# An attention mask taken off TensorE: GpSimd adds it to ScalarE's relu tile from step 5 on

## The chip, the cores and the metric

The kernel runs on one NeuronCore of one Trainium2 chip. The metric is the device time of one launch, in microseconds. Matmuls run on TensorE (PE), activations on ScalarE (ACT), elementwise work and reductions on VectorE (DVE) and GpSimd (POOL); SyncE (SP) issues the transfers.

## What is computed

128 graphs of 128 nodes with 256 features go through one graph attention layer (L0) and then a stack of three layers (L1), each attention, normalisation, a feed-forward of 256 to 1024 to 256, normalisation. The attention of L1 is, cut to what matters here:

```python
mask = adj + eye(n) > 0
scores = si[:, :, None] + sj[:, None, :] + attn_b[l]
scores = where(scores >= 0, scores, 0.2 * scores)
scores = where(mask, scores, -inf)
attn = softmax(scores, axis=-1)
agg = einsum('bij,bjd->bid', attn, x)
h = layernorm(x + agg, g1[l], beta1[l])
ff = gelu(h @ W1[l] + b1[l]) @ W2[l] + b2[l]
x = layernorm(h + ff, g2[l], beta2[l])
```

L0 has the same attention with the mask `adj == 0` and an elu behind it, between two residual sums.

## The kernel before

**Units and steps.** Four graphs form a group (T = 4; 32 groups), and a group in one of the three layers is a unit (96 units). Groups go in chunks of eight: eight groups in layer 0, the same in layer 1, then layer 2. So unit u has the layer u % 24 // 8. The program is one sequence of steps s from -6 to 97, each written by `body(st)` once for every engine; s = 24 to 71 is a hardware loop that turns twice over 24 steps. Each engine executes its own list in order; semaphores tie the lists together. Step s has the feed-forward of unit s and, around it, the attention of later units: the aggregation of unit s + 1, the scores and weights of unit s + 2, the row dots of unit s + 3, and the second normalisation of unit s - 1. The L0 work of a group is spread over four steps (`early`, `middle`, `late`, `end`); from group 8 on, `early` falls on every third step (s = 2, 5, 8, ... 71), `middle` on the next (3, 6, ... 72), `late` on the one after that. `only_middle(s)` is true in the steps of s % 3 == 0 from 3 to 72.

**The attention of a unit.** TensorE's `score_rows` turns the dots of the rows into a tile of sj in PSUM with four 128x128 fp32 transposes (L551) and adds the mask (0 or -2^100, bf16) with one matmul of the identity by the 128x512 mask tile (L553). ScalarE's `above` writes e = relu(4 (scores + si)) into SBUF (L724). VectorE's `row_lows` clears a column (L933), makes (scores + e) times -0.2 in PSUM and takes its minimum in each row (L936, four times). ScalarE's `exps` exponentiates from PSUM into e (L732); TensorE turns e (L559), and aggregates (L564). The leaky relu of score + si is 0.2 (x + relu(4x)) without the row's constant, which the softmax doesn't see.

**The feed-forward.** TensorE makes eight hidden blocks (`hidden(c)`, L588, six 128x512 matmuls each) in four PSUM banks. ScalarE takes the gelu twice (L859 rounded to g_hi, L861 in place), VectorE makes the remainder g_lo (`g_low(c)`, L983). Then TensorE makes the second product in four parts (`second(r)`, L605). The waits that tie them: `hidden(c)` for c >= 4 writes a bank again, and waits until its old block's g_lo is there; `turn = [0, 2, 3, 1, 2, 0, 3, 1]` gives the banks, so block 6 waits for g_lo 2 and block 7 for g_lo 3; and `second(0)` waits for g_lo c ahead of its block c.

**Order on the engines.** TensorE in a step: hidden(0), scores of s + 2, aggregation of s + 1 (L564), hidden(1), turn of L0's weights (if late), hidden(2), hidden(3), L0's scores (if middle), hidden(4) to (7), row turns (L646), second(0), second(1), L0's aggregation (if late), second(2), turn of e (L559), second(3). VectorE: g_low(0), row sums (L1037) and statistics, g_low(1), the variance (L968) of the first normalisation, `next_lows` (L933, L936), g_low(2), `first_norm` (L1074, waits for GpSimd's root), g_low(3), and so on to g_low(7), with the statistics of the input (in steps 2, 5, ...) and of vb (L957) in between; then low rows (L1108), shifts, and the row dots (L952). GpSimd: inverse root of the first normalisation (L1283), `scaled_rows` (L374, eight adds and products into hb), roots, the masks (`take_waits` L1278, then L1338 or L1347), L0's residual (L374 into elu_r), and last the affine part of unit s - 1 and, where its layer is the last, the residual (L374 into xo, 8 or 12 times). In steps 2, 5, ... that last part waits for the dots of the group (`dots0_ready`).

`take_waits(j)` is a one-column product into `spare` that takes up the waits ahead of a masking instruction. In steps 4 to 11 there are also pieces of late weights to split (`late_piece`).

Of the kernel before, what the change touches and what calls it, by code (L numbers as in the profile page):

```python
# [13 lines left out]
P = 128  # L14
T = 4
# [23 lines left out]
def build(nc, x, adj, w_fc, w_attn0, attn_w, attn_b, w1, b1, w2, b2, g1, beta1, g2, beta2, out):  # L39
# [25 lines left out]
    LATE = 4  # L65
    U = L * G
# [18 lines left out]
    with ctx:  # L85
# [27 lines left out]
        spare = sb("spare", [P, 4 + T])  # L113
# [111 lines left out]
        above_ready = sem("above_ready")  # L225
        low_ready = sem("low_ready")
# [38 lines left out]
        above0_ready = sem("above0_ready")  # L265
        low0_ready = sem("low0_ready")
# [55 lines left out]
        def early_norm(s):  # L322

            return s == -1

# [72 lines left out]
        def _(sp):  # L398
# [38 lines left out]
            def body(st):  # L437
# [90 lines left out]
        def _(pe):  # L528
# [18 lines left out]
            def score_rows(scores, mask, dot, done):  # L547


                for t in range(T):  # L550
                    pe.matmul(scores[:, t * P:(t + 1) * P], dot[:, 1, t:t + 1].to_broadcast((P, P)), ident[:, :],  # L551
                              is_transpose=True, start=(t == 0), stop=True, skip_group_check=True)
                pe.matmul(scores[:, :], ident_b[:, :], mask.rearrange("p t m -> p (t m)"),  # L553
                          start=False, stop=True, skip_group_check=True).then_inc(done, 1)
# [12 lines left out]
            def body(st):  # L567
# [51 lines left out]
                def next_scores():  # L619
                    if live(s + 2):  # L620
                        pe.wait_ge(dots_ready, st.nth(s + 2, 2 * T))
                        pe.wait_ge(m_in, 16 * st.nth(s + 2))
                        if live(s + 1):
                            pe.wait_ge(et_ready, st.nth(s + 1))
                        score_rows(ps_s, m1[s % 2][:, :, :], dots[s % 2], scores_ready)
# [6 lines left out]
                def first_scores():  # L632
                    if v1 is not None:
                        pe.wait_ge(dots0_ready, st.nth0(v1, 2 * T))
                        pe.wait_ge(masks0_ready, st.nth0(v1))
                        if v1:
                            pe.wait_ge(et0_ready, st.nth0(v1 - 1))
                        score_rows(ps_s0, m0[:, :, :], dots0, scores0_ready)
# [62 lines left out]
        def _(act):  # L701
# [40 lines left out]
            def body(st):  # L742
# [129 lines left out]
                next_exps()  # L872
                first_exps()
# [8 lines left out]
                second_norm()  # L882
# [8 lines left out]
        def _(dve):  # L891
# [37 lines left out]
            def row_lows(nth, u, taken, e, scores, lows, above_done, ready):  # L929


                dve.wait_ge(above_done, nth(u))
# [43 lines left out]
            def body(st):  # L976
# [9 lines left out]
                def first_lows():  # L986
                    if v1 is not None:
                        row_lows(st.nth0, v1, spare[:, 3 + T:4 + T], e0, ps_s0, low0, above0_ready, low0_ready)
# [56 lines left out]
                def first_variance():  # L1045
                    if live(s + 1):
                        if not live(s):
                            dve.tensor_copy(spare[:, 2:2 + T], neg_half[:, :])
# [38 lines left out]
                def input_variance():  # L1087
                    if v0 is not None:
                        if not live(s):
                            dve.tensor_copy(spare[:, 2:2 + T], neg_half[:, :])  # L1090
# [3 lines left out]
                def made_variance():  # L1094
                    if v3 is not None:
# [3 lines left out]
                        dve.tensor_copy(spare[:, 2:2 + T], neg_half[:, :])  # L1099
# [164 lines left out]
        def _(pool):  # L1264
# [38 lines left out]
            def body(st):  # L1303
# [29 lines left out]

                def mask():
# [33 lines left out]

                first_root()
# [49 lines left out]
```

## Time and profile before

| what | us |
|---|---|
| median of three runs | 2773.87 (2773.44 to 2774.45) |
| the profiled execution | 2771.33 |
| its span, first to last instruction | 2769.5 |
| TensorE busy | 2651.5 (96%), granted clock 0.985 |
| VectorE busy | 2138.1 (77%) |
| ScalarE busy | 2200.2 (79%) |
| GpSimd busy | 1689.8 (61%) |

The span holds all instructions of the profiled execution; 1.8 us of its time lie around it. Busy shares are means over the whole span, and matmuls overlap, so a sum of matmul durations is more than the busy time. In what follows a step begins at the first L588 matmul of its hidden(0): step 34 at 1073.70, 35 at 1102.14, 36 at 1129.11, 44 at 1350.04, 45 at 1377.32, 46 at 1405.22, 80 at 2338.39.

### The profile page before, as it was taken

How to read it: one execution, taken by the hardware profiler on the slowest of the kernel's cores; microseconds unless marked ns; L12 is line 12 of the kernel's file. 1: busy time of each engine (PE TensorE's matmuls, PEld its weight loads, DVE VectorE, ACT ScalarE, POOL GpSimd, SP SyncE). 2: the span in 40 equal slices, each digit the busy share in tenths (PEclk: the TensorE clock that was granted, in tenths of full speed). 3: DMA queues.
4: the chain of work that ended last, by engine and by line, in shares of the span. 5: the costliest groups of instructions: out<-in, count | busy, mean ns of one | idle time of the engine just before them, and what ended most of it. 6: DMA issues, size and time to landing. Idle time of an engine off the chain costs nothing.

```text
span 2769.5 us, 53308 instructions
## 1 busy us (share of the span) xinstructions
PE 2651.5 (96%) x16771; PEld 2386.7 (86%) x16868; DVE 2138.1 (77%) x7995; ACT 2200.2 (79%) x4494; POOL 1689.8 (61%) x2197
## 2 busy tenths in 40 slices
PE   3699999999999999999999999999999999999997
PEld 2488888988888989888888888889888998998997
DVE  5898878777878777878777878777878777676674
ACT  4699888888888888888887888888878777777774
POOL 4467666566766565566676666555677554454655
PEclk8699999999999999999999999999999999999999
DMA  5221322222222221122222122222222211111111
GB/s 177 90 70 62 95 81 92 66 79 76 87 81 77 66 71 62 64 70 88 85 90 69 65 67 76 69 68 68 80 89 91 62 45 52 35 52 52 51 64 54
DMA packets 118589, 203.43 MB, mean 73 GB/s; under 512 B 12800, under 2 KB 85536, under 8 KB 118304
## 3 DMA queue, kind: packets, MB, share of 16 engines
q1 hardware_dynamic: 118304, 199.97, 22.3%
q8 instruction: 137, 2.24, 0.3%
q14 instruction: 148, 1.21, 0.1%
HBM read 116.05 MB, written 83.89 MB: 72 GB/s over the span
## 4 chain that ended last, share of the span: by engine, by line
PE 71%; DVE 12%; POOL 8%; issue 5%; ACT 3%; DMA 0%; DVEq 0%; SPq 0%; POOLq 0%; ACTq 0%
PE bank L605 32%; PE bank L588 26%; PE ps_u L564 7%; POOL xo L374 3%; DVE g_lo L983 3%; DVE st L957 2%; PE ps_u L646 2%; POOL rs L1283 2%; DVE ub L1074 2%; PE ps_s L559 2%; PE ps_s L551 1%; POOL hb L374 1%; DVE vb L952 1%; DVE ub L952 1%; ACT g_hi L859 1%
## 5 line engine op out<-in xcount | busy, mean ns | idle before, releaser
L605 PE MATMUL bank<-w_hi,g_hi 128*128 128x256 f32 x3072 | 890.5, 290 | 15.3 <-DVE g_lo L983 15.1
L605 PE MATMUL bank<-w_hi,g_lo 128*128 128x256 f32 x3072 | 865.2, 282 | 0.0
L605 PE MATMUL bank<-w_lo,g_hi 128*128 128x256 f32 x3072 | 863.9, 281 | 0.0
L859 ACT ACTIVATE g_hi<-bank,b_eff 128x512 fp32r<-128x512 f32 x768 | 529.3, 689 | 334.4 <-PE bank L588 327.9
L983 DVE TENSOR_TENSOR g_lo<-bank,g_hi 128x512 fp32r<-128x512 f32 x768 | 518.9, 686 | 202.3 <-ACT bank L861 188.2
L588 PE MATMUL bank<-zt_hi,w_hi 128*128 128x512 f32 x1536 | 632.4, 412 | 12.0 <-DVE g_lo L983 5.6
L588 PE MATMUL bank<-zt_hi,w_lo 128*128 128x512 f32 x1536 | 607.7, 396 | 0.0
L588 PE MATMUL bank<-zt_lo,w_hi 128*128 128x512 f32 x1536 | 606.4, 395 | 0.0
L605 PEld LDWEIGHTS bank<-w_hi,g_hi 128*128 128x128 f32 x3072 | 578.9, 188 | 24.2 <-DVE g_lo L983 23.1
L605 PEld LDWEIGHTS bank<-w_lo,g_hi 128*128 128x128 f32 x3072 | 579.2, 189 | 0.8
L605 PEld LDWEIGHTS bank<-w_hi,g_lo 128*128 128x128 f32 x3072 | 578.7, 188 | 0.0
L1283 POOL TENSOR_TENSOR rs<-ve,neg_half 128x4 f32<-128x4 f32 x256 | 266.3, 1040 | 453.9 <-DVE ve L968 449.5
L861 ACT ACTIVATE bank<-bank,b_eff 128x512 f32<-128x512 f32 x768 | 508.4, 662 | 25.0
L374 POOL TENSOR_TENSOR xo<-xo,g_row 128x256 f32<-128x256 f32 x380 | 268.8, 739 | 201.4 <-ACT xo L739 139.7
L374 POOL TENSOR_TENSOR hb<-ub,g_row 128x256 f32<-128x256 f32 x384 | 272.5, 742 | 168.3 <-DVE ub L1074 168.2
L588 PEld LDWEIGHTS bank<-zt_hi,w_hi 128*128 128x128 f32 x1536 | 289.7, 189 | 78.7 <-DVE g_lo L983 10.9
L588 PEld LDWEIGHTS bank<-zt_hi,w_lo 128*128 128x128 f32 x1536 | 289.3, 188 | 68.0
L588 PEld LDWEIGHTS bank<-zt_lo,w_hi 128*128 128x128 f32 x1536 | 290.0, 189 | 60.3
L1180 DVE TENSOR_TENSOR vb<-bank,hb 128x512 f32<-128x512 f32 x192 | 129.9, 688 | 243.6 <-PE bank L605 215.4
L374 POOL TENSOR_TENSOR hb<-hb,bb_row 128x256 f32<-128x256 f32 x384 | 277.3, 754 | 7.5
L952 DVE CUSTOM_DVE_ANT_0 ub<-xb,aw_row 128x256 f32<-128x256 f32 x744 | 280.5, 432 | 1.2
L374 POOL TENSOR_TENSOR xo<-xo,beta_row 128x256 f32<-128x256 f32 x380 | 267.5, 735 | 7.5
(95 smaller groups left out, 4145.8 us busy)
## 6 DMA issues: line engine op xcount, KB each, us to landing
xb<-x_scratch SPq DMA_DIRECT2D x88, 512.0 KB, 4.0
x_scratch<-xo SPq DMA_DIRECT2D x64, 512.0 KB, 4.8
xin<-in_x SPq DMA_DIRECT2D x38, 512.0 KB, 5.9
r_scratch<-elu_r SPq DMA_DIRECT2D x32, 512.0 KB, 3.0
xin<-r_scratch SPq DMA_DIRECT2D x32, 512.0 KB, 4.6
out<-xo SPq DMA_DIRECT2D x32, 512.0 KB, 3.4
m<-m_scratch SPq DMA_DIRECT2D x96, 128.0 KB, 3.8
x_scratch<-h SPq DMA_DIRECT2D x24, 512.0 KB, 2.9
```

Source lines behind the costliest of these rows:

```text
L374: ins = eng.tensor_tensor(dst[:, t, :], src[:, t, :], other(t), op)
L559: mm = pe.transpose(dst[:, t * P:(t + 1) * P], e[:, t, :], ident[:, :])
L564: pe.matmul(sums[t // 2][:, t % 2 * D:(t % 2 + 1) * D], weights[:, t, :], rows[:, t, :], start=True, stop=True).then_inc(done, 1)
L588: mm = pe.matmul(bank[turn[c]][:, :], w[:, l, k, c * P:(c + 1) * P], z[:, k, :], start=(n == 0), stop=(n == 3 * K1 - 1))
L605: mm = pe.matmul(y, g[:, c, r * P:(r + 1) * P], w[:, l, c, :], start=(c == 0 and n == 0), stop=(c == C - 1 and n == 2))
L646: mm = pe.transpose(rows[k][:, t * P:(t + 1) * P], ub[:, t, k * P:(k + 1) * P], ident[:, :])
L859: act.activation(g_hi[:, c, :], block_in, ACT.Gelu, bias=bias).then_inc(g_hi_ready, 1)
L861: act.activation(block_in, block_in, ACT.Gelu, bias=bias).then_inc(gelu_done, 1)
L952: dve.tensor_tensor_reduce(junk[:, j, :], rows[:, t, :], vec(j), 1.0, 0.0, ALU.mult, ALU.add, dot[:, j, t:t + 1]).then_inc(ready, 1)
L983: dve.tensor_tensor(g_lo[:, c, :], bank[turn[c]][:, :], g_hi[:, c, :].bitcast(F32), ALU.subtract).then_inc(g_lo_ready, 1)
L1180: dve.tensor_tensor(vb[:, 2 * r:2 * r + 2, :], ps_y[r].rearrange("p (t d) -> p t d", d=D), hb[(s - 1) % 2][:, 2 * r:2 * r + 2, :], ALU.add ...
L1283: pool.tensor_tensor(rs[:, :], ve[:, :], neg_half[:, :], ALU.pow).then_inc(rs_ready, 1)
```

## The change

The mask matmul goes for the units from 7 and the L0 groups from 9 (scores made in step 5 or later). There `score_rows` ends with its last transpose, and GpSimd adds the mask tile to e behind ScalarE's relu, with a new semaphore `masked_ready` (`masked0_ready` for L0), for which VectorE's `row_lows` waits in place of `above_ready`. The value is the same, since (scores + e) is what is reduced, except that ps_s holds the sum with the mask only from `row_lows` on. GpSimd's instruction for the unit (`next_masked`) stands first in its step, ahead of `first_root`; the one for L0 (`first_masked`) stands behind the second and the input root. In steps of `only_middle`, ScalarE's `second_norm` moves ahead of `first_exps`, and VectorE's `first_lows` moves behind the first half of `next_dots`. `spare` is two columns wider. SyncE's load of the mask for unit s + 3 and GpSimd's own `first_mask` wait for the adds in place of the scores.

```diff
+    ASIDE = 5
+        def aside(u):
+            return u - 2 >= ASIDE
+        def aside0(v):
+            return early_step(v) + 1 >= ASIDE
+        ASIDE0 = min(v for v in range(G) if aside0(v))
...
                     if live(s + 1):
-                        sp.wait_ge(scores_ready, st.nth(s + 1))
+                        if aside(s + 1):
+                            sp.wait_ge(masked_ready, st.nth(s + 1 - 2 - ASIDE))
+                        else:
+                            sp.wait_ge(scores_ready, st.nth(s + 1))
...
-                pe.matmul(scores[:, :], ident_b[:, :], mask.rearrange("p t m -> p (t m)"),
-                          start=False, stop=True, skip_group_check=True).then_inc(done, 1)
+                if mask is not None:
+                    mm = pe.matmul(scores[:, :], ident_b[:, :], mask.rearrange("p t m -> p (t m)"),
+                                   start=False, stop=True, skip_group_check=True)
+                mm.then_inc(done, 1)
...
                 next_exps()
+                if only_middle(s) and not first_chunk:
+                    second_norm()
                 first_exps()
                 first_rows()
...
-                second_norm()
+                if not only_middle(s):
+                    second_norm()
                 make_rows()
...
                 def next_lows():
                     if live(s + 2):
-                        row_lows(st.nth, s + 2, spare[:, 2 + T:3 + T], e1, ps_s, low, above_ready, low_ready)
+                        taken = spare[:, 4 + T:5 + T]
+                        if aside(s + 2):
+                            row_lows(st.nth(s - ASIDE), taken, e1, ps_s, low, masked_ready, low_ready)
+                        else:
+                            row_lows(st.nth(s + 2), taken, e1, ps_s, low, above_ready, low_ready)
...
+                next_dots(range(T // 2))
                 if only_middle(s):
                     first_lows()
-                next_dots(range(T // 2))
                 made_variance()
...
+                def next_masked():
+                    if live(s + 2) and aside(s + 2):
+                        pool.wait_ge(above_ready, st.nth(s + 2))
+                        pool.wait_ge(m_in, 16 * st.nth(s + 2))
+                        take_waits(2)
+                        pool.tensor_tensor(e1[:, :, :], e1[:, :, :], m1[s % 2][:, :, :], ALU.add).then_inc(masked_ready, 1)
+
+                def first_masked():
+                    if v1 is not None and aside0(v1):
+                        pool.wait_ge(above0_ready, st.nth0(v1))
+                        pool.wait_ge(masks0_ready, st.nth0(v1))
+                        take_waits(3)
+                        pool.tensor_tensor(e0[:, :, :], e0[:, :, :], m0[:, :, :], ALU.add).then_inc(masked0_ready, 1)
...
-                        if v0:
+                        if v0 and aside0(v0 - 1):
+                            pool.wait_ge(masked0_ready, st.nth0(v0 - 1 - ASIDE0))
+                        elif v0:
                             pool.wait_ge(scores0_ready, st.nth0(v0 - 1))
...
+                next_masked()
                 first_root()
...
                     second_root()
                     input_root()
+                if only_middle(s):
+                    first_masked()
                 if v3 is not None and v3 >= CH:
                     made_root()
+                if not only_middle(s):
+                    first_masked()
                 mask()
                 first_mask()
```

## Rows read from the trace of the kernel before

**Rows 1.** The page, busy time, share of the span and instructions of each engine.

```profile
PE 2651.5 (96%) x16771; PEld 2386.7 (86%) x16868; DVE 2138.1 (77%) x7995; ACT 2200.2 (79%) x4494; POOL 1689.8 (61%) x2197
```

**Rows 2.** Windows, TensorE, steps 34, 35, 36, 44, 45, 80: from:to length, busy, clock.

```profile
1073.70:1102.14 28.44, 28.39 (x182) 1.00 0.13 38
1102.14:1129.11 26.97, 26.46 (x170) 1.00 0.30 94
1129.11:1156.01 26.90, 26.85 (x175) 1.00 0.22 75
1350.04:1377.32 27.28, 26.73 (x170) 1.00 0.35 111
1377.32:1405.22 27.90, 27.11 (x176) 1.00 0.28 91
2338.39:2364.67 26.28, 26.23 (x171) 1.00 0.15 46
```

**Rows 3.** Chain that ended last, step 45: start, duration, engine, tile, line.

```profile
1387.96 1.00 POOL rs L1283
...
1388.99 1.38 DVE ub L1074 x4
1390.37 0.61 DVE g_lo L983
...
1391.03 1.66 PE bank L588 x6
```

**Rows 4.** Groups of instructions, whole span: shapes, count, busy us, mean ns, idle before.

```profile
L374 POOL TENSOR_TENSOR xo<-xo,g_row 128x256 f32<-128x256 f32 x380 | 268.8, 739 | 201.4 <-ACT xo L739 139.7 <-DVE dots L952 49.2 <-issue 12.6
...
L1338 POOL TENSOR_SCALAR m_new<-m_new 128x512 bf16<-128x512 bf16 x32 | 62.3, 1948 | 2.2
...
L1278 POOL TENSOR_TENSOR spare<-neg_half 128x1 f32<-128x1 f32 x64 | 13.4, 209 | 14.6 <-DVE m_new L997 12.7 <-DMA adj_i<-in_adj 1.7
...
L553 PE MATMUL ps_s<-m,ident_b 128*128 128x512 bf16 x31 | 12.8, 412 | 0.0
...
L374 DVE TENSOR_TENSOR xo<-xo,g_row 128x256 f32<-128x256 f32 x4 | 1.4, 418 | 3.4 <-ACT xo L739 3.4
```

**Rows 5.** Timeline, TensorE, steps 36 and 46: start, duration, line, tiles.

```profile
1137.09 0.60 PE L551 MATMUL ps_s<-ident,dots 128*128 128x128 f32 x4
...
1137.97 0.39 PE L588 MATMUL bank<-zt_lo,w_hi 128*128 128x512 f32 x1
...
1410.40 0.60 PE L559 MATMUL ps_s<-ident,e 128*128 128x128 f32 x4
...
1411.07 0.39 PE L588 MATMUL bank<-zt_lo,w_hi 128*128 128x512 f32 x1
```

**Rows 6.** Timeline, GpSimd and VectorE, steps 44 and 45.

```profile
1355.65 2.83 POOL L374 TENSOR_TENSOR xo<-xo,xin 128x256 f32<-128x256 f32 x4 [0.16 <-POOL xo L374]
...
1358.42 0.29 DVE L936 CUSTOM_DVE_ANT_0 ps_s<-ps_s,e 128x128 f32<-128x128 f32 x1
...
1385.15 2.81 POOL L374 TENSOR_TENSOR xo<-xo,xin 128x256 f32<-128x256 f32 x4 [0.16 <-POOL xo L374]
...
1385.83 0.29 DVE L936 CUSTOM_DVE_ANT_0 ps_s<-ps_s,e 128x128 f32<-128x128 f32 x1
...
1386.78 0.68 DVE L983 TENSOR_TENSOR g_lo<-bank,g_hi 128x512 fp32r<-128x512 f32 x1
```

**Rows 7.** Timeline, GpSimd, VectorE and ScalarE, steps 35 and 36.

```profile
1104.78 2.81 POOL L374 TENSOR_TENSOR xo<-xo,beta_row 128x256 f32<-128x256 f32 x4
...
1110.19 0.30 DVE L936 CUSTOM_DVE_ANT_0 ps_s<-ps_s,e 128x128 f32<-128x128 f32 x1
...
1132.01 1.13 ACT L724 ACTIVATE e<-ps_s,si 128x128 f32<-128x128 f32 x4
...
1134.07 2.82 POOL L374 TENSOR_TENSOR xo<-xo,beta_row 128x256 f32<-128x256 f32 x4
...
1137.35 0.30 DVE L936 CUSTOM_DVE_ANT_0 ps_s<-ps_s,e 128x128 f32<-128x128 f32 x1
```

More of the change, by code:

```diff
@@ L112, in build @@
         neg_half = sb("neg_half", [P, T])
-        spare = sb("spare", [P, 4 + T])
+        spare = sb("spare", [P, 6 + T])
         xb = [sb(f"xb{i}", [P, T, D]) for i in range(2)]
@@ L225, in build @@
         above_ready = sem("above_ready")
+        masked_ready = sem("masked_ready")
         low_ready = sem("low_ready")
@@ L265, in build @@
         above0_ready = sem("above0_ready")
+        masked0_ready = sem("masked0_ready")
         low0_ready = sem("low0_ready")
@@ L550, in score_rows @@
                 for t in range(T):
-                    pe.matmul(scores[:, t * P:(t + 1) * P], dot[:, 1, t:t + 1].to_broadcast((P, P)), ident[:, :],
-                              is_transpose=True, start=(t == 0), stop=True, skip_group_check=True)
-                pe.matmul(scores[:, :], ident_b[:, :], mask.rearrange("p t m -> p (t m)"),
-                          start=False, stop=True, skip_group_check=True).then_inc(done, 1)
+                    mm = pe.matmul(scores[:, t * P:(t + 1) * P], dot[:, 1, t:t + 1].to_broadcast((P, P)), ident[:, :],
+                                   is_transpose=True, start=(t == 0), stop=True, skip_group_check=True)
+                if mask is not None:
+                    mm = pe.matmul(scores[:, :], ident_b[:, :], mask.rearrange("p t m -> p (t m)"),
+                                   start=False, stop=True, skip_group_check=True)
+                mm.then_inc(done, 1)
             def turn_weights(dst, e, done):
@@ L621, in next_scores @@
                         pe.wait_ge(dots_ready, st.nth(s + 2, 2 * T))
-                        pe.wait_ge(m_in, 16 * st.nth(s + 2))
+                        if not aside(s + 2):
+                            pe.wait_ge(m_in, 16 * st.nth(s + 2))
                         if live(s + 1):
                             pe.wait_ge(et_ready, st.nth(s + 1))
-                        score_rows(ps_s, m1[s % 2][:, :, :], dots[s % 2], scores_ready)
+                        score_rows(ps_s, None if aside(s + 2) else m1[s % 2][:, :, :], dots[s % 2], scores_ready)
                 def first_turn():
@@ L634, in first_scores @@
                         pe.wait_ge(dots0_ready, st.nth0(v1, 2 * T))
-                        pe.wait_ge(masks0_ready, st.nth0(v1))
+                        if not aside0(v1):
+                            pe.wait_ge(masks0_ready, st.nth0(v1))
                         if v1:
                             pe.wait_ge(et0_ready, st.nth0(v1 - 1))
-                        score_rows(ps_s0, m0[:, :, :], dots0, scores0_ready)
+                        score_rows(ps_s0, None if aside0(v1) else m0[:, :, :], dots0, scores0_ready)
                 def row_turns():
@@ L927, in rows, with row_lows @@
                 link(dve.tensor_scalar(beta2_row[:, L - 1, :], beta2_row[:, L - 1, :], -1.0, None, ALU.add))
-            def row_lows(nth, u, taken, e, scores, lows, above_done, ready):
-                dve.wait_ge(above_done, nth(u))
+            def row_lows(done, taken, e, scores, lows, above_done, ready):
+                dve.wait_ge(above_done, done)
                 dve.memset(taken, 0.0)
@@ L987, in first_lows @@
                     if v1 is not None:
-                        row_lows(st.nth0, v1, spare[:, 3 + T:4 + T], e0, ps_s0, low0, above0_ready, low0_ready)
+                        taken = spare[:, 5 + T:6 + T]
+                        if aside0(v1):
+                            row_lows(st.nth0(v1 - ASIDE0), taken, e0, ps_s0, low0, masked0_ready, low0_ready)
+                        else:
+                            row_lows(st.nth0(v1), taken, e0, ps_s0, low0, above0_ready, low0_ready)
                 junk = ub if s >= 0 else vb
@@ L1047, in first_variance @@
                         if not live(s):
-                            dve.tensor_copy(spare[:, 2:2 + T], neg_half[:, :])
+                            dve.tensor_copy(spare[:, 4:4 + T], neg_half[:, :])
                         moments(st1, mv1, mv1_ready)
@@ L1053, in next_lows @@
                     if live(s + 2):
-                        row_lows(st.nth, s + 2, spare[:, 2 + T:3 + T], e1, ps_s, low, above_ready, low_ready)
+                        taken = spare[:, 4 + T:5 + T]
+                        if aside(s + 2):
+                            row_lows(st.nth(s - ASIDE), taken, e1, ps_s, low, masked_ready, low_ready)
+                        else:
+                            row_lows(st.nth(s + 2), taken, e1, ps_s, low, above_ready, low_ready)
                 def next_heads():
@@ L1089, in input_variance @@
                         if not live(s):
-                            dve.tensor_copy(spare[:, 2:2 + T], neg_half[:, :])
+                            dve.tensor_copy(spare[:, 4:4 + T], neg_half[:, :])
                         moments(st4, mv4, mv4_ready)
@@ L1098, in made_variance @@
                         dve.wait_ge(st3_ready, st.nth0(v3))
-                        dve.tensor_copy(spare[:, 2:2 + T], neg_half[:, :])
+                        dve.tensor_copy(spare[:, 4:4 + T], neg_half[:, :])
                         moments(st3, mv3, mv3_ready)
```

## The prediction, made before the change was run

> **What bounds the kernel now.** I read the page's busy shares first: TensorE 96%, GpSimd 61% [rows 1]. That looks like a TensorE bound with a half idle GpSimd, which would make every removed matmul a gain. The share is a mean over unlike steps, so I cut the trace at the first matmul of each step and looked at single steps [rows 2]. Steps go by s modulo 3 while first-layer work runs (s up to 73). Class 1 (s = 34) is 28.44 us with TensorE busy 28.39: TensorE-bound. Class 0 (s = 36) is 26.90, 26.85 busy. Class 2 (s = 35) is 26.97, 26.46 busy: it waits half a microsecond. The eight steps of class 0 that follow a last-layer unit (s = 45) are 27.90 with 27.11 busy. The 20 plain steps from s = 74 (s = 80 shown) are 26.28, 26.23 busy. So in class 2, and in class 0 at times, something else sets part of the end.
>
> The chain of waits in step 45 names it [rows 3]: GpSimd's inverse root (L1283), VectorE's norm (L1074), VectorE's low half g_lo (L983), then TensorE's last hidden block. Before the root, GpSimd is still in the affine and the residual of unit 43, left over from the step before: the last xo ends at 1385.15 + 2.81 = 1387.96, and the root begins then [rows 3, 6]. This is exactly the place where the change puts its new instruction.
>
> **What goes.** 89 units (7 to 95) and 23 first-layer groups (9 to 31) lose one 128x512 bf16 matmul, 112 in all. Its record is 412 ns [rows 4], but matmuls overlap. The same four transposes without a mask matmul behind them (L559) hold the stream from 1410.40 to the second hidden matmul at 1411.07, 0.67 us; with it (L551) from 1137.09 to 1137.97, 0.88 us [rows 5]. The difference, 0.21 us, is what I take; 0.41, the whole record, is the upper bound, and nothing is the lower.
>
> **What comes.** A one-column multiply on GpSimd (209 ns) and a 128x512 add with fp32 and bf16 inputs, which the trace doesn't show. A 128x256 add takes 739 ns and the one-column one 209 [rows 4], so 530 ns for 255 columns, 2.08 ns each; 512 columns give 0.21 + 511 x 2.08 = 1.27 us. The other 128x512 bf16 operation on GpSimd takes 1948 ns, but applies two operations with constants. Bounds: 0.74, the add of half the columns, and 1.95; I take 1.27, because kind and first operand are those of the add. In the trace a 128x512 operation behind the one-column multiply starts about 0.23 us after what stood before. So the masked tile is ready 0.23 + 1.27 + 0.03 (a semaphore) = 1.53 us after GpSimd is free and the relu is done; relu ends at 1133.14, 4.03 us into step 36 [rows 7], and at nearly the same offset in the others, which is earlier than matters.
>
> The Trainium skill (GPSIMD Engine Reference, section 3.1) puts a two-input operation at about 2.6 cycles per element of 1.2 GHz: by it, as an estimate, 1.11 us for 512 columns, and the sum below would be some 5 us lower. Its section 4.1 speaks against the change: elementwise arithmetic belongs on VectorE, GpSimd being about twice as slow; the trace agrees, 418 ns against 739 for the same affine add [rows 4].
>
> **Who waits.** VectorE reduces the row minima (L936) in order between variance and g_lo block 2; all later g_lo blocks and the norm stand behind it. The inverse root now stands behind the add on GpSimd. TensorE's hidden block 6 needs g_lo 2, block 7 needs g_lo 3, the second product's last part needs g_lo 7 (the waits in low_done). Class by class, time into the step of "GpSimd free + 1.53" against the first L936:
> - Class 1 (s = 7 to 73, 23 steps) and the 20 plain ones: GpSimd is free at 6.0 or before, the minima begin at 8.0. Hidden; TensorE-bound, 0.21 gained each: 43 x 0.21 = -9.0 us.
> - Class 2 after layers 0 and 1 (s = 35 and eleven like it): free at 1104.78 + 2.81 = 1107.59, ready at 1109.12, minima at 1110.19 [rows 7]. Hidden. These steps end by g_lo 7, whose chain has only 0.15 us of waiting on ScalarE in it: -0.15 each, -1.8. Steps 14 and 17: 0.
> - Class 0 there (s = 36, ten more; here VectorE's dots let GpSimd start only 2 us into the step): free at 1136.89, ready at 1138.42 against 1137.35 [rows 7]: 1.07 late, and so are the norm and g_lo 3. Hidden block 7 has 0.5 of slack before and the two masks give 0.42 more: +0.1 each, +1.1.
> - Class 2 after a last-layer unit (20, 23, 44, 47, 68, 71): free at 1355.65 + 2.83 = 1358.48, ready at 1360.01 against 1358.42 [rows 6]: 1.59 late. g_lo 7 sets the end already: +1.58 each, +9.5.
> - Class 0 after a last-layer unit (18, 21, 24, 42, 45, 66, 69, 72): free at 1387.96, ready at 1389.49. The chain [rows 3] was root 1.03, then norm. Now it is add 1.53, four minima 0.95 (1385.83 to 1386.78 [rows 6]), g_lo 2 0.60, norm: norm at 1391.04 instead of 1388.99, the root hidden beside it. +2.05 each, +16.4. Step 48, delayed by the loop's turn, +0.7.
> - Six steps of the first chunk (5, 6, 8, 9, 11, 12), where GpSimd also makes late weight halves and is free at 7.0 to 9.8: by the same subtraction 0.6, 0.5, 2.3, 0.5, 2.3, 1.2: +7.4.
>
> Sum: -9.0 - 1.8 + 1.1 + 9.5 + 16.4 + 0.7 + 7.4 = +24.3 us. The profiled execution took 2771.3 (span 2769.5); the median of the runs is 2773.9, 2.5 above. 2773.9 + 24.3 = **2798 us**, 0.9% slower.
>
> **The moved parts.** In class 0 steps the first-layer add stands behind the second root (which ends at 18.5 into step 36): done at 20.0, while VectorE has four of the moved dots (0.35 each) to do until 20.2. Nothing. ScalarE's normalisation of vb moves ahead of the first-layer exponentials: those end as late as before, and their tile is wanted only in the next step; xo comes 1.4 us sooner, so GpSimd is earlier in class 1, which has room. If that cover were gone, 0.3 us in 23 steps, 7 us. On SyncE's queue the mask load for s + 3 now waits for the add of s + 1, made a step before; the load lands in some 4 us with a step to spare. GpSimd's own first-layer mask waits for an add it did itself. Nothing.
>
> **Rivals.**
> - A slow add: the bf16 input makes it cost 1.95 as L1338 does [rows 4]. For it: the same size and type. Against: another operation. 0.68 us more in the 32 steps in which it is on the chain: +22, **2820 us**.
> - TensorE is the bound and the add hides (the other sign): 112 x 0.21 = 23.5 us less, **2750 us**. For it: 96% busy, and GpSimd idle 39%. It decides if GpSimd is free before 6.5 us into the step everywhere; in 32 steps of 89 the trace says it isn't [rows 3, 6, 7]. It needs an order of GpSimd's work other than the one that I read.
> - Gains and waits cancel: the removed matmul is worth its 0.41 us (43 x 0.20 = 9 us more) and TensorE's waits are half of what I count (15 less): about **2774 us**. For it: the slack of class 0, where g_lo 3 is late by less than 0.5. Against: the steps after the last layer, where TensorE already waits.
>
> **How the numbers follow.** Chances: forecast 0.62, slow add 0.22, hidden 0.10, cancelled 0.06. 0.2% (5.5 us) is about what a measurement of this kernel can tell from no change. Faster 0.11, same 0.05, slower 0.84. The forecast's own range is 2788 to 2808 (0.41 for the matmul below, unseen delays above). For 8 in 10 it must reach to the slow add and its own spread, and on the other side to an add of 0.74 (0.53 less in 32 steps, 17 us, 2781): 2780 to 2824; the hidden case stays outside.
>
> **What the profile after would show.** The add at 1.2 to 1.4 us; idle time ahead of L936 put down to GpSimd's e, near 1.6 us in steps like 44 and 3.6 in steps like 45; TensorE idle at hidden blocks 6 and 7 there, these steps at 28.9 and 29.9 us; classes 1 and plain at 28.2 and 26.0. I am wrong if steps like 45 stay at 27.9: then VectorE isn't held by the add. If they are at 30.6, the add is the slow one. If plain steps stay at 26.3, the matmul was free. TensorE would idle up to 2.7 us in a piece before hidden block 6; all six steps of rows 2 have the clock granted in full, and a fall of it there would be one more surprise on the slow side.

## The result, and the profile after

The kernel after takes 2802.99 us (median of four runs, 2801.72 to 2805.15), the kernel before 2773.65 beside it on the same chip (2771.57 to 2774.45): a ratio of 1.0108, interval 1.009 to 1.0125. That is slower, by 29.3 us, 5 us more than forecast and inside its range. One run of all those below lay apart, an execution of experiment 12 with 3314.27 us at a granted clock of 0.748, and no comparison here uses it. The page of the profiled execution, span and busy times:

```profile
span 2802.3 us, 53531 instructions
...
PE 2665.0 (95%) x16748; PEld 2380.8 (85%) x16756; DVE 2187.7 (78%) x7995; ACT 2202.0 (79%) x4494; POOL 1839.6 (66%) x2421
```

TensorE has 112 matmuls less to do (the weight loads PEld are 112 fewer than in [rows 1]; the profile has records of only 31 of the 128 mask matmuls before and of 8 of the 16 after) and is busy for 13.5 us **longer** than before. No term of the prediction's sum makes it so; this is the first sign of a missing one. The groups that answer to [rows 4], and those of the minima and the dots:

```profile
L975 DVE CUSTOM_DVE_ANT_0 ub<-xb,aw_row 128x256 f32<-128x256 f32 x744 | 306.7, 468 | 3.4 <-issue 1.6
...
L959 DVE CUSTOM_DVE_ANT_0 ps_s<-ps_s,e 128x128 f32<-128x128 f32 x512 | 133.1, 321 | 45.0 <-issue 44.7
...
L1370 POOL TENSOR_TENSOR e<-e,m 128x512 f32<-128x512 f32 x89 | 104.0, 1169 | 0.0
...
L1309 POOL TENSOR_TENSOR spare<-neg_half 128x1 f32<-128x1 f32 x176 | 39.7, 225 | 79.3 <-ACT e L744 64.2 <-DVE m_new L1024 12.3 <-DMA adj_i<-in_adj 2.1
...
L1377 POOL TENSOR_TENSOR e<-e,m 128x512 f32<-128x512 f32 x23 | 26.8, 1167 | 0.0
```

The add (L1370) takes 1.17 us, 0.10 less than the forecast's 1.27. VectorE now idles 45.0 us ahead of the minima (L959), where it idled 6.2 us before. The profile puts 44.7 of it down to "issue", that is to no engine, and not to GpSimd's e as the prediction expected; that it is the add that ends it is read from the order in time below, and tested by experiments 8 and 11. Windows of the steps of [rows 2] (34, 35, 36, 44, 45, 80), TensorE; the fourth figure is the granted clock:

```profile
1089.88:1118.24 28.36, 28.36 (x183) 1.00 0.11 38
1118.24:1145.08 26.84, 26.47 (x170) 1.00 0.30 95
1145.08:1171.86 26.78, 26.78 (x174) 1.00 0.21 74
1367.10:1395.81 28.71, 27.25 (x170) 1.00 0.35 106
1395.81:1426.60 30.79, 28.45 (x174) 0.94 0.25 82
2371.22:2397.43 26.21, 26.21 (x170) 1.00 0.14 46
```

Step 44 grew by 1.43 us and step 45 by 2.89, as the mechanism says. But step 34 shrank by only 0.08 and step 80 by only 0.07, where 0.21 was forecast; and in step 45 the clock is at 0.94. Timeline of step 45, GpSimd and VectorE:

```profile
1406.31 0.19 POOL L1309 TENSOR_TENSOR spare<-neg_half 128x1 f32<-128x1 f32 x1
1406.45 1.15 POOL L1370 TENSOR_TENSOR e<-e,m 128x512 f32<-128x512 f32 x1
1407.57 1.03 POOL L1314 TENSOR_TENSOR rs<-ve,neg_half 128x4 f32<-128x4 f32 x1
...
1407.64 0.29 DVE L959 CUSTOM_DVE_ANT_0 ps_s<-ps_s,e 128x128 f32<-128x128 f32 x1 [3.36 <-issue]
...
1409.20 1.37 DVE L1105 TENSOR_SCALAR ub<-ub,mv,rs 128x256 f32<-128x256 f32 x4
```

The residual of unit 43 ends at 1406.34; the add, the minima and then the norm follow one behind the other, while the root runs hidden beside the minima. The norm comes 13.39 us into the step against 11.67 before [rows 3]. TensorE's hidden blocks in the same stretch:

```profile
1406.60 0.40 PE L606 MATMUL bank<-zt_hi,w_lo 128*128 128x512 f32 x1
1409.34 0.50 PE L606 MATMUL bank<-zt_hi,w_hi 128*128 128x512 f32 x1 [2.34 <-DVE g_lo L1006]
...
1410.39 0.63 PE L606 MATMUL bank<-zt_hi,w_hi 128*128 128x512 f32 x1
1410.82 0.63 PE L606 MATMUL bank<-zt_lo,w_hi 128*128 128x512 f32 x1
```

Behind the wait the matmuls start 0.43 us apart, where they start 0.23 apart elsewhere. The windows around it show why:

```profile
1406.60:1409.30 2.70, 0.40 (x2) 1.00 0.80 218
1410.00:1412.90 2.90, 2.90 (x8) 0.50 0.23 92
1413.00:1415.00 2.00, 2.00 (x15) 0.94 0.00 0
```

TensorE did nothing for 2.34 us, and the granted clock then stood at 0.50, which is 1.2 GHz, for some 3 us. In the kernel before it stands at 1.00 from step 1 to step 94.

Up to the start of step 95 the kernel after is 32.4 us later than before, 31.7 of it in the 95 steps, and the spans differ by 32.8; the medians differ by 29.3, since the profiled execution of before lies 2.3 under its median and that of after 1.2 above its own.

### The profile page after: what moved, and what is told of

Its sections match the earlier page's. It is cut to its first block, busy times and chain, and to the rows that moved or that the text cites. A ratio compares the mean times of both kernels' runs of the same rounds, so it can differ in the third digit from the quotient of the medians.

```text
span 2802.3 us, 53531 instructions
## 1 busy us (share of the span) xinstructions
PE 2665.0 (95%) x16748; PEld 2380.8 (85%) x16756; DVE 2187.7 (78%) x7995; ACT 2202.0 (79%) x4494; POOL 1839.6 (66%) x2421
## 3 DMA queue, kind: packets, MB, share of 16 engines
q8 instruction: 137, 2.24, 0.3%
q14 instruction: 151, 1.24, 0.1%
## 4 chain that ended last, share of the span: by engine, by line
PE 71%; DVE 16%; issue 6%; POOL 4%; ACT 3%; DMA 0%; DVEq 0%; SPq 0%; POOLq 0%; ACTq 0%
PE bank L623 33%; PE bank L606 27%; PE ps_u L582 6%; DVE st L980 4%; DVE g_lo L1006 3%; PE ps_u L666 2%; DVE ub L1064 2%; PE ps_s L577 2%; POOL rs L1314 2%; DVE ub L1105 1%; DVE ub L975 1%; PE ps_s L567 1%; DVE vb L975 1%; POOL hb L387 1%; DVE ps_s L959 1%
## 5 line engine op out<-in xcount | busy, mean ns | idle before, releaser
L606 PE MATMUL bank<-zt_hi,w_hi 128*128 128x512 f32 x1536 | 639.5, 416 | 35.5 <-DVE g_lo L1006 28.1
L623 PEld LDWEIGHTS bank<-w_hi,g_hi 128*128 128x128 f32 x3072 | 578.7, 188 | 23.8 <-DVE g_lo L1006 22.8
L975 DVE CUSTOM_DVE_ANT_0 ub<-xb,aw_row 128x256 f32<-128x256 f32 x744 | 306.7, 468 | 3.4 <-issue 1.6
```

The source lines that it names most:

```text
L606: mm = pe.matmul(bank[turn[c]][:, :], w[:, l, k, c * P:(c + 1) * P], z[:, k, :], start=(n == 0), stop=(n == 3 * K1 - 1))
L623: mm = pe.matmul(y, g[:, c, r * P:(r + 1) * P], w[:, l, c, :], start=(c == 0 and n == 0), stop=(c == C - 1 and n == 2))
L975: dve.tensor_tensor_reduce(junk[:, j, :], rows[:, t, :], vec(j), 1.0, 0.0, ALU.mult, ALU.add, dot[:, j, t:t + 1]).then_inc(ready, 1)
```

## The experiments

Each ran 4 to 11 times, against the kernel before on the chip of the experiment. The chips differ; the kernel before has medians of 2773.65, 2773.80, 2773.89 and 2774.28 us on them, so times of different experiments compare to within about half a microsecond. Where steps are compared, the profiled executions are.

**1. Only the wider `spare`.** The suspicion was that the two new columns cost something: they move every tile that is allocated behind `spare` (g_hi, g_lo, zt_hi, zt_lo, e, the inputs) and not the weights ahead of it. The kernel before with that one line of the diff:

```diff
-        spare = sb("spare", [P, 4 + T])
+        spare = sb("spare", [P, 6 + T])
```

> The kernel before with one edit: the scratch tile spare is 6 + T columns wide in place of 4 + T, so that every tile allocated behind it (g_hi, g_lo, zt_hi, zt_lo, e1, xb, hb) moves by 8 bytes in each partition. Nothing else. Theory (the move slows TensorE's operand reads): in the kernel after every matmul of the two products starts 1.2 ns later behind the one before it than in the kernel before (0.11987 for 0.11864 us, and 0.23389 for 0.23274), even in steps 1 and 4 that the change doesn't touch; 13,824 such matmuls by 1.2 ns is 16.6 us. Then this kernel is some 16 us slower than before, near 2790. Rival (the spacing differs from run to run or comes with the rest of the change): no difference, 2774.

2785.47 us (2783.41 to 2787.11), ratio 1.0043 (1.003 to 1.0057): **11.7 us of the 29.3 have nothing to do with the mask.** 16 were expected, from slower starts of all matmuls of the two products; but where TensorE waits anyway they cost next to nothing (0.4 us in the 14 steps behind a last-layer unit together). Windows of steps 34, 45 and 80:

```profile
1077.55:1106.12 28.57, 28.52 (x183) 1.00 0.13 38
...
1382.41:1410.34 27.93, 27.28 (x176) 1.00 0.27 91
2347.61:2374.04 26.43, 26.38 (x171) 1.00 0.15 46
```

Against these, the steps 34 and 80 of the kernel after are 0.21 and 0.22 us shorter: the matmul is worth what was forecast, in both.

**2 and 3. Both kernels with `spare` at 12 + T** (the diff is that of the kernel after; the kernel before has 4 + T there). 4 + T columns are 32 bytes, 12 + T are 64. Both expectations took it that 6 + T had moved the later tiles by 8 bytes and that a multiple of 32 bytes would undo the harm.

```diff
-        spare = sb("spare", [P, 6 + T])
+        spare = sb("spare", [P, 12 + T])
```

> The kernel after with spare 12 + T columns wide (64 bytes; 4 + T were 32), so that the tiles behind it stand again on addresses that are multiples of 32 bytes. Theory of the move: the spacing goes back to 0.1187, and of the 29 us that the change cost 16 go: near 2787. Rival: nothing changes, 2803.

> The kernel before with spare 12 + T columns wide: the same alignment to 32 bytes as before, all tiles behind moved by 32 bytes. Theory of the move (what matters is the alignment, not the place): 2774, as before. If it is the place alone, it moves by some us.

After: 2805.39 us, ratio 1.0114 (1.0098 to 1.0129). Before: 2784.74, ratio 1.0039 (1.0026 to 1.0053). Both expectations missed, 2787 and 2774: the times are those with 6 + T. By the addresses in the built programs, tiles are laid out in slots of 32 bytes, so that 6 + T take 64 bytes as 12 + T do, and both move the later tiles by 32. No run lists the addresses; the equal times agree with it. At equal places the mask costs 17.5 us (the kernel after against experiment 1) to 20.7 (experiment 2 against 3).

**4. The add only where it is covered.** In steps 13 to 93, but with the matmul kept in class 0 and in class 2 behind a last-layer unit while first-layer work runs (L0's masks stay on GpSimd); `spare` 12 + T. The count that the waits use is made anew for it (not shown):

```diff
         def aside(u):
-            return u - 2 >= ASIDE
+            s = u - 2
+            busy = s < U - PER + 2 and (s % 3 == 0 or (s % 3 == 2 and 18 <= s % PER))
+            return 13 <= s < U - 2 and not busy
```

> The kernel after, spare 12 + T wide, and the mask of a unit goes to GpSimd only in the steps where GpSimd is free early enough: all of class 1 from 13, class 2 except those after a last-layer unit, and the plain ones from 74. In class 0, in steps 20, 23, 44, 47, 68, 71 and before 13 TensorE adds the unit's mask as before. The first-layer masks stay on GpSimd. My account of the change (the add delays VectorE's minima where GpSimd comes late; elsewhere it hides and the matmul's 0.21 us are gained): gain in 41 TensorE-bound steps 8.6 us, in 14 steps of class 2 about 2, in the class 0 steps after layers 0 and 1 the first-layer matmul, 0.2 in 12, 2.4: near 2761, and no step of class 0 above 27.9. Rival (the matmul is worth next to nothing, as the plain steps of the kernel after suggest with 0.03 us): 2770 to 2774. Second rival (the first-layer add delays something too): above 2774.

2773.02 us (2770.97 to 2774.7), ratio 0.9996 (0.9987 to 1.0005). The expectation of 2761 us missed, and the time by itself is that of its first rival (the matmul is worth nothing). Experiment 1 decides, whose tiles lie in the same places: against it the time is 12.4 us less, where the parts of the expectation add up to 13, and class 1 from step 13 and the plain steps are 0.21 us shorter each. The gain is real where GpSimd is free, and the moved tiles eat it.

**5 and 6. Both kernels with the later tiles 64 bytes on** (`spare` at 20 + T).

> The kernel before with spare 20 + T columns wide. Tiles are laid out in slots of 32 bytes: with 4 + T columns the tiles behind spare (g_hi, g_lo, zt_hi, zt_lo and all later ones) start at multiples of 64 bytes, with 6 + T or 12 + T at 32 behind one, with 20 + T again at multiples of 64. Theory (TensorE's operands want a start at a multiple of 64): spacing of the matmuls back at 0.1187 and 0.2327, 2774. Rival (any place other than the first is slower): 2785, as with 6 + T and 12 + T.

> The kernel after with spare 20 + T wide. By the same theory the change loses the 11 us that the two wider spares cost the kernel before, and what is left is the change proper: near 2792, 18 us over before. Rival: 2803.

Before: 2762.72 us (2762.18 to 2763.07), ratio 0.996 (0.9946 to 0.9974), faster than the kernel before by 11 us with nothing but an address changed. Neither the theory (2774) nor its rival (2785) has that: this place isn't as good as the first, it is better. After: 2787.73 (2787.33 to 2790.03), ratio 1.0052 (1.0039 to 1.0066); 2792 was expected. Windows of steps 44 and 45, first of 5, then of 6:

```profile
1349.03:1376.40 27.37, 26.65 (x171) 1.00 0.35 111
1376.40:1404.00 27.60, 26.81 (x176) 1.00 0.27 92
```

```profile
1361.66:1390.42 28.76, 27.03 (x170) 1.00 0.34 106
1390.42:1421.12 30.70, 28.11 (x174) 0.94 0.26 82
```

At this place the mask costs 25.0 us: the same two kinds of steps grow by the same amounts (1.39 and 3.10 here).

**7. Experiments 4 and 5 together:** the add where it is covered, `spare` at 20 + T.

> e4_covered_steps (the unit's mask on GpSimd only where GpSimd is free in time) with spare 20 + T wide. Theory: e4 stood at before's time only because the place of the tiles took back what the removed matmuls gave; with it mended 2773 - 11 = 2762, faster than both kernels, and plain steps at 26.05. Rival (the matmul is worth nothing even so): 2771 to 2774.

2753.72 us (2750.64 to 2754.12), ratio 0.9928 (0.9915 to 0.9942): 20 us faster than the kernel before, 49 faster than the kernel after, and 8 under the expectation, which took 11 us for the way from 32 to 64 bytes, where experiments 1 and 5 lie 22.8 apart. Of the 20 us, 11.2 are the place (experiment 5) and 9.0 the mask.

**8. A later add.** Experiment 6 with four more one-column products on GpSimd ahead of the unit's add. By the timeline of step 45 the five products take 0.77 us in place of 0.19, and the add and the minima are late by 0.58.

```diff
+                        for j in range(8, 12):
+                            take_waits(j)
                         pool.tensor_tensor(e1[:, :, :], e1[:, :, :], m1[s % 2][:, :, :], ALU.add).then_inc(masked_ready, 1)
```

> e6_after_64 with four more one-column products on GpSimd ahead of the unit's add, which makes the masked tile about 0.65 us later in every step and leaves all else. Theory (GpSimd's lateness stands on the chain in classes 0 and 2 behind a last-layer unit, 15 steps, in the six steps of the first chunk, and past its slack in eleven others of class 0; it is hidden in the rest): 0.65 in 21 steps, 14 us, and some 0.5 in 11, 5 us: 19 us over e6. Rival (the lost time is a fixed cost of another kind, the clock's fall or the moved parts): under 5 us over e6.

2812.03 us (2810.65 to 2814.18), ratio 1.0139 (1.0123 to 1.0155), 24.3 more than experiment 6, where 19 were expected. The chain is the one described: classes 1 and plain don't move (0.7 and 0.0 us in 44 steps together), class 2 behind a last-layer unit moves by 0.54 in the mean, the six early steps by 0.59, and the other steps of class 0 by 0.64 (0.02 to 1.12 in single steps): in the mean their slack was used up. The eight steps of class 0 behind a last-layer unit move by 0.96 in the mean, but between -0.70 and +2.91, with where the clock fell: in 18, 21, 24, 42, 69 and 72 here, in 21, 45, 66 and 69 in experiment 6. Steps 44 and 45:

```profile
1377.47:1406.77 29.30, 27.04 (x171) 1.00 0.33 105
1406.77:1436.77 30.00, 26.63 (x175) 1.00 0.26 84
```

Step 45 starts its add later than in experiment 6 and is 0.70 us **shorter**, since here its clock didn't fall. So the fall costs about 0.58 + 0.70 = 1.3 us where it comes, an estimate from one pair of steps; in steps 8 and 11, where it also fell here, it cost nothing that shows (they grew by 0.58 and 0.59). It comes in some steps and not in others, and the length of the wait alone doesn't decide it: here TensorE waits 3.14 us in step 45 without a fall, and 1.82 us in step 11 with one.

**9. Everything moved by 64 bytes, the weights too**: a 64-byte tile ahead of all.

```diff
+        first = sb("first", [P, 16])
```

> The kernel before with a 64-byte tile of its own allocated ahead of everything, so that the weights and all later tiles start 64 bytes further on, with no distance between them changed. Moving only the tiles behind `spare` by 64 bytes gave 2762.7 us and matmuls of the second product 0.1167 us apart, against 2773.9 and 0.1186. Theory A, the time of a matmul goes with the absolute start address of its moving operand (the g and zt tiles): 2763 us and 0.1167 us again. Theory B, it goes with the distance between the weight tile and the moving tile: nothing changes, 2774 us and 0.1186 us. Theory C, the weights' own start address counts with its own effect: neither of the two times.

2773.28 us (2772.47 to 2774.96), ratio 1.0 (0.9991 to 1.0009), and 89 of the 95 steps have the length of before within 0.06 us. Of the three theories B holds, for a move of 64 bytes: what counts is how the tiles on the two sides of `spare` lie to each other, not where they all lie. (My expectation calls g the moving operand of the second product; in the rows g is what the array holds and w2 moves. It decides nothing here, since all move.)

**10 and 12. The kernel before with the later tiles 96 and 128 bytes on** (`spare` at 28 + T and 36 + T).

> The kernel before with `spare` 24 columns wider, so that the tiles behind it start 96 bytes further on. Moved by 0, 32 and 64 bytes they gave 2773.9, 2785.1 and 2762.7 us, with second-product matmuls 0.1186, 0.1199 and 0.1167 us apart. If the effect is one of the start within 64 bytes (an odd multiple of 32 bytes costs), 96 behaves as 32: about 2785 us and 0.1199 us. If each of the four starts within 128 bytes has a time of its own, the result is another one; nothing measured so far says which, and anything from 2755 to 2790 us is open.

> The kernel before with `spare` 32 columns wider, so that the tiles behind it start 128 bytes further on. If the effect of the start address repeats every 128 bytes, the time is that of the kernel before, 2774 us, with second-product matmuls 0.1186 us apart. If it repeats at 256 bytes or more, or goes with a distance to tiles that are not moved, the time is another one.

2762.61 us (2760.75 to 2764.07), ratio 0.9961 (0.9948 to 0.9975); and 2772.05 (2770.02 to 2772.43), ratio 0.9993 (0.9984 to 1.0003). At 96, 2785 was expected; that an odd multiple of 32 costs is refuted. The time at 128 is within 2 us of before, as expected if the effect repeats every 128 bytes, but by another sum: the hidden matmuls are quicker and the second product's slower, so a period of 128 bytes isn't shown. Mean time from start to start of neighbouring matmuls, worked out over each whole trace (starts under 0.26 and under 0.15 us apart), and the mean length of the plain steps 74 to 93:

| later tiles moved by | time, us | hidden, ns | second product, ns | plain steps, us |
|---|---|---|---|---|
| 0 (before) | 2773.7 | 232.7 | 118.6 | 26.26 |
| 32 (experiment 1) | 2785.5 | 233.9 | 119.9 | 26.43 |
| 64 (experiment 5) | 2762.7 | 233.4 | 116.7 | 26.05 |
| 96 (experiment 10) | 2762.6 | 233.0 | 116.9 | 26.08 |
| 128 (experiment 12) | 2772.1 | 228.2 | 119.8 | 26.19 |
| all tiles by 64 (experiment 9) | 2773.3 | 232.7 | 118.7 | 26.26 |

A step has 48 hidden matmuls and 96 of the second product. For 32 bytes that makes 48 x 1.12 + 96 x 1.24 = 173 ns (differences before rounding), and the plain steps are 0.17 us longer. In the timeline of step 84 the first and the last of 72 matmuls on end, first of the kernel before (8.51 us apart), then of experiment 5 (8.14):

```profile
2457.79 0.36 PE L605 MATMUL bank<-w_hi,g_hi 128*128 128x256 f32 x1
...
2466.30 0.28 PE L605 MATMUL bank<-w_hi,g_lo 128*128 128x256 f32 x1
```

```profile
2451.33 0.36 PE L605 MATMUL bank<-w_hi,g_hi 128*128 128x256 f32 x1
...
2459.47 0.28 PE L605 MATMUL bank<-w_hi,g_lo 128*128 128x256 f32 x1
```

The duration of each record is the same. Only the starts tell, which is why no group of instructions shows it. But step 84 is one of the good ones of experiment 5. Its plain steps alternate, 25.88 us when s is even and 26.21 when it is odd, and in step 85 the same 72 starts span 8.45 us:

```profile
2477.23 0.36 PE L605 MATMUL bank<-w_hi,g_hi 128*128 128x256 f32 x1
...
2485.68 0.28 PE L605 MATMUL bank<-w_hi,g_lo 128*128 128x256 f32 x1
```

The mean of 116.7 ns is one of 114.4 and 117.8. Both steps read the same tiles g and w2 at the same places and write the same banks, so the distance between TensorE's own operands can't be the whole cause. Tiles that other engines read and write do alternate with s (xb, the mask, the dots); that these play a part was not tested.

**11. The add ahead of the residual.** Experiment 6, but in the 15 steps behind a last-layer unit GpSimd makes the add between the affine part and the residual of the step before.

```diff
-                next_masked()
+                if not masked_early(s):
+                    next_masked(s + 2)
...
+                    if masked_early(s + 1):
+                        next_masked(s + 3)
```

> The changed kernel with its tiles moved to the 64-byte start (2787.7 us), and in the 15 steps behind a last-layer unit (classes 0 and 2) GpSimd makes the unit's masked add at the tail of the step before, ahead of the residual of that step, not behind it. My theory says that those steps are long because the masked tile waits for affine and residual on GpSimd: then the minima no longer wait, the norm in steps like 45 comes near 12.8 us into the step and TensorE's wait before hidden block 6 falls from 2.3 us to under 1.5, and no step shows the clock at half. Class 0 steps then cost about 1.1 us over the kernel before and not 1.9 to 3.5, class 2 ones 0.6 and not 1.4: about 17 us less, near 2771 us. Rival: the delay comes from VectorE's own order (minima ahead of g_lo), whatever GpSimd's order is: no change, 2788 us. A middle result, over 2778 us, would say that the residual, now later, is wanted by something that I have not counted.

2775.95 us (2773.08 to 2780.27), ratio 1.0008 (0.9999 to 1.0017): 11.8 us less by the medians, 16.5 by the spans of the profiled executions (2787.8 and 2771.3). That refutes the rival (2788). Of the 16.5, 14.0 lie in the 15 steps that the edit changes, and 2.9 before step 5, where it changes nothing: in step 2 the clock fell in experiment 6 and not here. 17 was forecast. The eleven runs of this kernel spread over 7 us. Timeline of step 45 (from 1383.00), then windows of its hidden blocks:

```profile
1390.82 1.17 POOL L1374 TENSOR_TENSOR e<-e,m 128x512 f32<-128x512 f32 x1
1391.01 1.02 DVE L995 TENSOR_SCALAR ve<-mv 128x4 f32<-128x4 f32 x1
1391.94 2.84 POOL L391 TENSOR_TENSOR xo<-xo,xin 128x256 f32<-128x256 f32 x4
...
1392.04 0.29 DVE L963 CUSTOM_DVE_ANT_0 ps_s<-ps_s,e 128x128 f32<-128x128 f32 x1
...
1395.81 1.38 DVE L1109 TENSOR_SCALAR ub<-ub,mv,rs 128x256 f32<-128x256 f32 x4 [2.13 <-POOL rs L1318]
...
1397.85 0.79 PE L610 MATMUL bank<-zt_hi,w_hi 128*128 128x512 f32 x1 [2.29 <-DVE g_lo L1010]
```

```profile
1395.00:1397.00 2.00, 0.56 (x3) 1.00 0.61 209
...
1398.00:1399.00 1.00, 1.00 (x3) 0.50 0.95 385
```

The minima come at 9.04 us into the step (12.02 in experiment 6), and the norm at 12.81, as expected. VectorE shows no idle time ahead of the minima, but its variance (L995) ahead of them took 1.02 us and ended 0.03 us behind the add, so a wait for GpSimd can hide in an instruction's duration. The part of the expectation on the clock was a miss: block 6 no longer waits, but block 7 now waits 2.29 us for g_lo 3 behind the norm, and the clock fell in steps 18 and 45 (and at the start of step 48, the loop's turn, where it also fell in experiments 3 and 6). The other seven steps of this kind are 0.4 to 1.5 us over experiment 5, these two 2.6 and 2.8.

## Why the prediction came out as it did

Its terms against the traces. The first measured column compares the kernel after with experiment 1, so with the later tiles in the same places; the last compares experiments 6 and 5. Sums over the steps, us.

| term | forecast | at 32 bytes | at 64 bytes |
|---|---|---|---|
| class 1 (23) and plain (21) | -9.0 | -9.1 | -5.7 |
| class 2, others (14) | -1.8 | -2.4 | -2.9 |
| class 0, others (11) | +1.1 | -3.0 | -0.7 |
| class 2 behind a last-layer unit (6) | +9.5 | +8.4 | +8.3 |
| class 0 behind a last-layer unit (8) | +16.4 | +19.5 | +21.3 |
| step 48 | +0.7 | +0.8 | +1.0 |
| the six of the first chunk | +7.4 | +4.8 | +4.8 |
| sum | +24.3 | +19.0 | +26.1 |
| steps 0 to 4 and what lies before | none | +1.7 | +0.4 |
| the moved tiles (experiment 1 against before) | none | +11.7 | |

Of the +1.7, 1.4 is step 2, where the clock fell in the kernel after and not in experiment 1.

- **The step that failed is one that isn't there.** The diff says that `spare` becomes two columns wider, and the prediction gave that no price. It costs 11.7 us, 40% of the result. That the sum came near is luck: the terms that are there were 5 us too high at this place of the tiles, and the missing one was larger; without it the same kernel would have been about 2791 to 2794, as worked out from the medians and from the steps. Steps 34 and 80 said so: they fell by 0.07 to 0.08, not 0.21. The prediction's own test, "If plain steps stay at 26.3, the matmul was free", read that sign wrongly: the matmul is worth 0.21 (experiment 1), and the rest is paid in slower starts of all the others.
- **The removed matmul: right,** 0.21 us in steps 34 and 80 against experiment 1. At 64 bytes the plain steps alternate between +0.1 and -0.2, because those of experiment 5 do (25.88 and 26.21 us) while those of experiment 6 are nearly equal (25.97 and 26.00). So the gain isn't the same at every place.
- **The add: a little too dear.** 1.17 us for 1.27, and it starts 0.11 behind the end of the residual in step 45, not 0.23. In step 45 the minima begin 1.30 us behind the end of the residual, forecast 1.53. The slow add is out: the bf16 input costs nothing visible here. By the 2.6 cycles per element of the Trainium skill (GPSIMD Engine Reference, section 3.1) the estimate was 1.11 us; the measured 1.17 is nearer to it than to my 1.27.
- **Class 2 behind a last-layer unit: right.** VectorE's idle time ahead of the minima is 1.28 us in step 44 (forecast 1.6), step 44 is 28.71 (forecast 28.9). Experiment 11 moved the add ahead of the residual, and 4.7 of the 8.3 us went.
- **Class 0 behind a last-layer unit: the mechanism right, the clock not counted.** Idle 3.36 us (forecast 3.6), norm +1.72 (forecast +2.05). Four of the eight steps grew by 1.85 to 2.24 against before, where 2.05 was forecast. The other four (21, 45, 66, 69) grew by 2.89 to 3.16: these are the ones with the clock at half. That is 4 x about 1.1 us more, the "surprise on the slow side" that the prediction named and didn't price. With the add ahead of the residual (experiment 11) 8.8 of the 21.3 us went.
- **The first chunk and the other class 0 steps: too high.** In step 36 the minima are 0.64 us later than before, not 1.07, since GpSimd came free 0.2 earlier and the add is quicker; the slack of block 7 took that. The other steps of class 0 were forecast at +0.1 each and got shorter by 0.27. By experiment 8, at the 64-byte place, 0.58 us more of delay costs 0.64 in the mean of these steps: little slack is left there.
- **The moved parts: nothing, as said.** Class 1 shows its full 0.21 behind them.
- **The rivals.** That the add hides everywhere is refuted by steps 44 and 45; it holds in 44 steps, and experiment 4 shows what a kernel gets that makes the add only in such places. "Gains and waits cancel" had the matmul at 0.41; it is 0.21.

What stays open: between which tiles the distance counts, and why. Experiment 9 shows that what counts is how tiles lie to each other across `spare`. The weights lie on one side and g and zt on the other, and the starts of their matmuls change, but so do the places of all the tiles that the other engines use, no run moved one tile alone, and the alternation in experiment 5 speaks against TensorE's operands as the whole cause. Which steps the clock falls in was not settled either: a wait of 2.34 us precedes the fall in step 45, and one of 2.34 us precedes none in step 42. In experiment 2, the same kernel with the later tiles in the same places, it is the other way about: the clock fell in steps 18, 21, 42, 66, 69 and 72 and not in 45, behind waits of 2.29 to 2.69 us. Timeline of the kernel after, TensorE, step 42, where the matmuls behind the wait stay 0.24 us apart:

```profile
1322.55 0.50 PE L606 MATMUL bank<-zt_hi,w_hi 128*128 128x512 f32 x1 [2.34 <-DVE g_lo L1006]
1322.88 0.40 PE L606 MATMUL bank<-zt_lo,w_hi 128*128 128x512 f32 x1
1323.12 0.40 PE L606 MATMUL bank<-zt_hi,w_lo 128*128 128x512 f32 x1
```

## What to carry to other kernels

A busy share of 61% says nothing on whether one more instruction fits: ask in each kind of step what the engine still owes at the moment when the new instruction should run, and put it only where it owes nothing. Make every comparison of two kernels at equal addresses: one resized scratch tile was worth 11 to 12 us either way, as much as the 12.4 that the add gained in experiment 4, and trying another place for it costs one line. When a change makes TensorE wait longer in a piece, look at the granted clock behind the wait and count a fall as a cost of its own: here a fall came behind waits of 1.8 to 3.3 us, in some steps and not in their likes.

## What the runs showed of the hardware

**Places of tiles to each other.** The table above: 2762.6 to 2785.5 us for the same instructions. The Trainium skill (SBUF — State Buffer, Operand start alignment) says of its rules on where an operand may start: "This is about legality, not speed". It times nothing; these runs show that where tiles lie does change how fast these fp32r matmuls start one behind the other (114.4 to 119.9 ns apart in the second product), though not by an operand's start alone.

**Instructions of VectorE that stood still for GpSimd's add.** VectorE's dots (L975, two SBUF inputs) went from 432 to 468 ns in the mean. It isn't spread over all. Timeline of step 36 in the kernel after, GpSimd and VectorE:

```profile
1164.32 1.17 POOL L1377 TENSOR_TENSOR e<-e,m 128x512 f32<-128x512 f32 x1
...
1164.47 1.30 DVE L975 CUSTOM_DVE_ANT_0 ub<-xb,aw_row 128x256 f32<-128x256 f32 x1
1165.70 0.41 DVE L975 CUSTOM_DVE_ANT_0 ub<-xb,aw_row 128x256 f32<-128x256 f32 x1
```

A dot that starts while the L0 add runs takes 1.30 us and not 0.42, ending 0.28 behind it. The minima, with one operand in PSUM, take their usual 0.29 in experiment 11 while GpSimd's residual runs. The Trainium skill (SBUF — State Buffer, SBUF: two separate sides) says that VectorE with two SBUF inputs and GpSimd share a pair of ports that is an exclusive lock for a whole instruction; by that rule, the trace agrees, with 0.88 us of standing still. Here it was hidden.

The variance stood as well, and it reads one tile of 128x4. It takes 0.17 us in step 36 of the kernel before; in the kernel after it ends 0.02 us behind the unit's add (1152.76 + 1.16):

```profile
1152.94 1.00 DVE L991 TENSOR_SCALAR ve<-mv 128x4 f32<-128x4 f32 x1
```

**The granted clock** fell to 0.50 behind a wait of 2.34 us in step 45. It fell in or shortly behind the wait in four of the eight steps with such a wait (waits of 2.28 to 2.71 us), in six of the eight in experiments 2 (2.29 to 2.69) and 8 (3.05 to 3.30), and in two of the eight in experiment 11, behind block 7 (2.29 to 2.46). A fall also came behind 1.82 and 1.84 us in steps 11 and 8 of experiment 8.
